# Expert outputs delivered to token order, and indirect DMAs in pairs by scan step, in a macaron block of mixture of experts and delta-rule attention

## The reference

```python
x = x + 0.5 * ffn(layernorm(x))
x = x + attn(layernorm(x))
x = x + 0.5 * ffn(layernorm(x))
```

```python
p, idx = top_k(softmax(x @ gate_w.T), 2);  p = p / sum(p)
for k in range(2):
    pos = place of the token in the queue of expert idx[:, k]   # by token number
    valid = pos < capacity                                      # 640
    disp = zeros(8, 640, 128) filled with the valid tokens
    y = (silu(disp @ wi_gate.T) * (disp @ wi_up.T)) @ wo.T      # hidden width 512
    out += where(valid, p[:, k] * y[idx, pos], 0)
```

## Time and profile before

| | |
|---|---|
| median of 3 runs | 1117.05 us (1116.97, 1117.05, 1122.63) |
| the profiled execution | 1120.73 us, of which its span is 1118.9 |
| mean granted TensorE clock | 0.898 of the full 2.4 GHz |
| busy PE / DVE / ACT / POOL | 854.6 / 543.9 / 335.9 / 465.5 us |
| routing | 0 to 75 us |
| `e1` | 75 to 299 us, PE busy 202.9, clock 0.97 |
| attention, stage -1 | 299 to 405 us |
| stages 0, 1, 2 | to 505, 610 and 715 us, PE busy 98 to 102 in each |
| stage 3 and the last routing | 715 to 845 us |
| `e2` | 845 to 1060 us, PE busy 201.1, clock 0.95 |
| `collect` | 1060 to 1119 us, DVE busy 17.2, POOL 39.5, PE none |

### The profile page before, as it was taken

How to read it: one execution, slowest core, us unless ns; L and a number is a source line. 1 busy time by engine, 2 the same in 40 slices (tenths; PEclk the granted TensorE clock), 3 DMA queues, 4 the chain that set the end, 5 groups by cost and what they waited for, 6 DMA issues and landing times. The chain is left out here.

```text
span 1118.9 us, 26929 instructions
## 1 busy us (share of the span) xinstructions
PE 854.6 (76%) x11563; PEld 751.8 (67%) x11563; DVE 543.9 (49%) x1569; ACT 335.9 (30%) x646; POOL 465.5 (42%) x588
## 2 busy tenths in 40 slices
PE   4419999969558579988998899797526999799800
PEld 3419999969546457776777678665415999799800
DVE  6715565625455024575566356622623555445333
ACT  2214444324122112342234325311413444334200
POOL 1664479842233820870185028302024420323076
PEclk9999999979868869999999999986656999989955
DMA  7333434523100000000000000000004434334113
GB/s 266 131 109 112 142 116 125 157 88 94 56 26 2 0 22 4 2 20 32 4 2 21 4 4 1 21 4 21 1 17 139 133 125 136 107 118 143 55 40 110
DMA packets 68467, 75.71 MB, mean 68 GB/s; under 512 B 8150, under 2 KB 55165, under 8 KB 67836
## 3 DMA queue, kind: packets, MB, share of 16 engines
q1 hardware_dynamic: 60156, 57.27, 16.2%
...
## 5 line engine op out<-in xcount | busy, mean ns | idle before, releaser
L237 POOL DMA_INDIRECT queue<-xn,slot x128 | 128.2, 1002 | 247.8 <-DVE slot L1459 104.7
L638 DVE TENSOR_TENSOR e_hid<-e_sg,e_pu 128x320 f32<-128x320 f32 x256 | 123.9, 486 | 195.8 <-ACT e_sg L594 134.1
L594 ACT ACTIVATE e_sg<-e_pg 128x320 f32<-128x320 f32 x256 | 111.6, 438 | 233.1 <-PE e_pg L556 162.4
L554 PE MATMUL e_pg<-e_xlo,e_whi 128*128 128x320 f32 x256 | 97.7, 382 | 23.6 <-issue 15.3
L243 POOL DMA_INDIRECT xn<-rows,slot x64 | 61.6, 963 | 123.2 <-ACT e_xhi L580 61.1
L684 POOL TENSOR_TENSOR a_prod<-a_inv,a_nmat 128x31 f32<-128x31 f32 (+15 forms) x124 | 64.5, 521 | 95.4 <-DVE a_nmat L1317 86.0
L541 PE MATMUL e_po<-expert,e_hid 128*128 128x128 f32 x640 | 86.2, 278 | 0.3 <-issue 0.3
L541 PE MATMUL e_po<-e_expert,e_hid 128*128 128x128 f32 x640 | 84.0, 276 | 1.3 <-DVE e_hid L638 1.3
L895 PE MATMUL a_pz<-a_vhi,lag_hi 128*128 128x512 f32 x184 | 79.3, 431 | 5.0 <-DVE a_vlo L1272 5.0
L541 PEld LDWEIGHTS e_po<-expert,e_hid 128*128 128x128 f32 x640 | 82.2, 194 | 0.5 <-issue 0.5
L541 PEld LDWEIGHTS e_po<-e_expert,e_hid 128*128 128x128 f32 x640 | 80.3, 193 | 1.8 <-DVE e_hid L638 1.8
...
## 6 DMA issues: line engine op xcount, KB each, us to landing
...
queue<-xn,slot POOLq DMA_INDIRECT x128
```

The costliest lines, as they stand in the source:

```text
L237: pool.indirect_dma_start(io.queue[c], bass.IndirectOffsetOnAxis(ap=k.slot[:, j, c:c + 1], axis=0), k.xn[:, j, :], None, bounds_check=SLOT ...
L554: pe.matmul(out, whi[par][:, i, fs], xlo[par][:, cols], start=True, stop=False)
L594: act.activation(sg[n % 2][:], pg[n % 2][:, 0:HALF], ACT.Silu).then_inc(silued, 1)
L638: dve.tensor_tensor(hid[q % 2][:, f, c * HALF:c * HALF + HALF], sg[n % 2][:], pu[n % 2][:, 0:HALF], ALU.mult).then_inc(hidden, 1)
```

## The change

**What it does.** The queue rows get a 129th number, the token's own number (less a constant, so that an empty slot, which holds zeros, is out of bounds). VectorE turns that column of `xs` into a table `token` for each pass (`index`). Where the next reader wants token order, `deliver` writes the expert's output rows by token number into `io.token[c]`, five indirect DMAs for a pass, and rows with a number out of bounds are skipped. In `e1` that is done for choice 1, in `e2` for both. They are read back by plain loads: four of 512 KB in attention, and eight at the end of `e2`. The choice-0 rows of `e1` still go to `io.rows` in slot order and are gathered: group 0 in `e1`, four tiles before pass 8's deliveries and four behind them, group 1 and 2 at the head of attention, group 3 in pairs in stage 0. `token[0]` and `token[1]` are zeroed by SP, as are the queues.

The folding of attention's weights is cut into pieces that stand between the groups of scatters in `e1`. In `e2` only the last group's eight choice-1 scatters are left in the loops; attention sends the other 24 along with choice 0. The last pass projects the pass before it down two blocks earlier, and its own first two tiles in between, each tile copied out by itself. The first inversion moves to VectorE. `collect` as a function goes; its adds and stores stand at the end of `e2`.

```diff
-def gather(pool, io, c, slot, dst, got):
-    pool.indirect_dma_start(dst, None, io.rows[c], bass.IndirectOffsetOnAxis(ap=slot, axis=0)).then_inc(got, 16)
+def gather(pool, io, slot, dst, got):
+    pool.indirect_dma_start(dst, None, io.rows, bass.IndirectOffsetOnAxis(ap=slot, axis=0)).then_inc(got, 16)
+def deliver(pool, io, c, token, src, stored):
+    pool.indirect_dma_start(io.token[c], bass.IndirectOffsetOnAxis(ap=token, axis=0), src, None,
+                            bounds_check=NTOK - 1, oob_is_err=False).then_inc(stored, 16)
...
-                clear(sp, 1, later)
-            sp.wait_ge(later, 16 * (1 + (len(loads) + CLEARS if raw else 0)))
+                for table in (io.queue[1], io.token[1], io.token[0]):
+                    clear(sp, table, later)
+                sp.dma_start(io.rows[SLOTS:SLOTS + 1, :], zero[0:1, 0:D]).then_inc(later, 16)
...
+                dve.tensor_copy(k.xn[:, :, D], k.const[:, C_TOKEN:C_TOKEN + NT])
...
-        SCATTERS = (0, 5, 10, 15, 20, 24, 28, NT)
+        SCATTERS = (0, 5, 10, 15, 20, 24, 28, NT) if raw else (NT - GRP, NT - GRP // 2, NT)
+        NSENT = SCATTERS[-1] - SCATTERS[0]
+        LAST = NQ - 1
+        BY_TOKEN = (1,) if raw else (0, 1)
...
+            def collect(c, g):
+                own = slice(g * GRP, (g + 1) * GRP)
+                dst = second[:, own, :] if c else k.xn[:, own, 0:D]
+                sp.dma_start(dst, io.token[c].rearrange("(n p) d -> p n d", p=P)[:, own, :]).then_inc(got[c][g // 2 if c else 0], 16)
...
+                    if q == LAST:
+                        if n < CT:
+                            down(q - 1, n)
+                        elif n < CT + 2:
+                            down_last(n - CT)
+                    elif q and n in DOWN_AT:
                         down(q - 1, DOWN_AT.index(n))
-            for s in range(CT):
-                down(NQ - 1, s)
+            for s in range(2, CT):
+                down_last(s)
...
+            def index(q):
+                dve.tensor_scalar(token[:, q, :], xs[q % 2][:, :, D], float(NUMBERED), None,
...
+                if raw and i == 1:
+                    raw.fold_taps(pool, k, folded)
+                if raw and i == 2:
+                    raw.split_taps(pool, k, folded)
+                if raw and i == 3:
+                    raw.split_gates(pool, k, stacked)
+                if raw and i == 4:
+                    raw.fold_far(pool, k)
+                if raw and i == 5:
+                    raw.fold_near(pool, k)
...
+            def send_rows(q):
+                c = q // E
+                pool.wait_ge(indexed, numbered(q))
+                for s in range(CT):
+                    pool.wait_ge(rready, 2 * q + (s if q == LAST else s // 4) + 1)
+                    deliver(pool, io, c, token[:, q, s:s + 1], rows[q % 2][:, s, :], stored[c][q % 2])
...
+            pool.wait_ge(sent, 16 * NSENT)
+            if raw:
+                all_stored(pool, 0)
+                fetch(0, GRP // 2)
+            for q in range(NQ):
+                if q // E in BY_TOKEN:
+                    send_rows(q)
+                if raw and q == E:
+                    fetch(GRP // 2, GRP)
...
+            rows = io.token[1].rearrange("(n p) d -> p n d", p=P)
+            for a in range(NGRP):
+                own = slice(a * GRP, (a + 1) * GRP)
+                sp.dma_start(k.xn[:, own, 0:D] if a else second, rows[:, own, :]).then_inc(loaded[min(a, 1)], 16)
...
             fetch(1)
-            for g in range(-1, NGRP):
-                if g + 1 < NGRP:
-                    invert(g + 1)
-                if g >= 1:
-                    send(g - 1)
-                if g + 3 < NGRP:
-                    fetch(g + 3)
-            send(NGRP - 1)
-            pool.wait_ge(sent, 16 * NT)
+            fetch(2)
+            invert(0)
+            for j in range(4):
+                in_step(0, j + 1)
+                fetch(3, 2 * j, 2 * j + 2)
+            invert(1)
+            invert(2)
+            for j in range(4):
+                in_step(2, j)
+                send(0, 0, 2 * j, 2 * j + 2)
+                behind_read(2, j + 1)
+                send(0, 1, 2 * j, 2 * j + 2)
+            invert(3)
+            for j in range(4):
+                in_step(3, j)
+                send(1, 0, 2 * j, 2 * j + 2)
+                behind_read(3, j + 1)
+                send(1, 1, 2 * j, 2 * j + 2)
+            for j in range(4):
+                in_step(3, j + 4)
+                send(2, 0, 2 * j, 2 * j + 2)
+                if j < 3:
+                    behind_read(3, j + 5)
+                    send(2, 1, 2 * j, 2 * j + 2)
+            send(2, 1, 6, GRP)
+            send(NGRP - 1, 0)
...
+            def invert_first(first, last):
+                dve.wait_ge(subchain, 2)
+                dve.wait_ge(factored, 1)
+                substitute(dve, link, nmat, inv, prod, first, last)
+                if last == CHUNK - 1:
+                    dve.sem_inc(inverted, 1)
...
+                if ahead and not here and n == 4:
+                    low_values(a, 0)
+                    low_values(a, 1)
+                    invert_first(0, 12)
+                    cross_values(a)
+                    invert_first(12, CHUNK - 1)
...
-            for a in range(NGRP):
-                combine(a, 0)
+            link(dve.tensor_scalar(k.xn[:, :, D], k.xn[:, :, D], -float(APART), None, ALU.add))
+            combine(0, 0)
...
+        self.queue = [scratch(f"queue{c}", SLOTS, ROW) for c in range(TOPK)]
+        self.rows = scratch("rows", SLOTS + 1, D)
+        self.token = [scratch(f"token{c}", NTOK, D) for c in range(TOPK)]
```

261 lines of the change are left out of this document (158 added, 103 removed).

## The result

The changed kernel takes **1087.18 us** (median of 4, 1085.01 to 1089.70) where the kernel before takes 1117.82 beside it. The ratio is 0.9711, 95% interval 0.9683 to 0.9739. The forecast was 1040, its range 1020 to 1066. The profiled execution took 1089.70 with a span of 1087.7, 31.2 less than the 1118.9 of before.

A forecast was written before the change was run, and what follows sets the result against it. Bound: TensorE in the experts, stalled under long rows of indirect DMAs, then 32 gathers at the end. -23 - 3 - 20 - 4 - 28 + 1.4 = -76.6 from 1120.73: 1044.1; that execution lay 3.7 above median, so 1040, range 1020 to 1066.

The forecast's parts named there:

- Four places, one pattern: Both expert phases, a scan read in attention and two solves: long rows of indirect DMAs run TensorE dry, 4 to 12 us in.
- Five in a row, 6.5 us, cost nothing: Expert passes: five scatters in a row leave TensorE busy 11.83 of 12 us, so they cost nothing.
- D: Attention: last stage's burst goes, scatters stand in pairs by scan step; -4 us, bounds -8 and +20.
- A: Experts' interiors: both 16-bursts go, five deliveries per by-token expert replace them; -13.05 - 8.96 - 2.10 + 1 = -23 us.
- F: Queue rows of 516 bytes instead of 512: first load of each expert phase grows; 2 x 0.7 = +1.4 us.
- B: First experts to attention: next stage starts 4.1 us later, but attention's head gets shorter; -3 us together.
- E: Tail: 32 gathers and their wait go; deliveries, plain loads and adds replace them, one delivery held; -28 us.
- The head: Start of attention: one 512 KB load replaces waiting for eight gathers; adds done at 311.0 against 313.86.
- C: First inversion moves to VectorE (-11), two solves no longer under gathers (-8), less time at 1.2 GHz (-1); -20 us.
- pairs starve the scan: Rival, 15%: 48 scatters in attention's scan steps lose 24 us at half the old burst's rate, giving 1062; at all, 1084.
- the better case: Rival, 20%: tail deliveries not held (5.7 us), stage 3 loses nothing (4 more), a little from bursts; 1026.
- It decides from 2.4 us for a delivery: Rival, slower, 2%: GpSimd bounds the 24 delivering experts, 120 us per us above that; at 3.1 all 77 is lost.

The follow-up runs named there:

- e1: Not a follow-up run: the kernel's first expert phase (sublayer), which ends where attention begins; no measured time of its own as a run.

## Why the prediction was wrong

**What bounds the kernel.** "Four places, one pattern: a long unbroken row of indirect DMAs, and TensorE runs dry some 4 us into it": the pattern was seen rightly in that trace, and it is real in the late condition. Two things in it were wrong. It is the other engines that take up TensorE's results late, which the rows of the changed kernel show, so an engine can be hit with large instructions and in a short row. And "Five in a row, 6.5 us, cost nothing" was read from a busy share of 11.83 in 12 us. From the first scatter of that row, at 109.89, to the first of the next, at 122.59, it is 12.70 in the same trace, and the next pass, with four, 12.02. A busy share over a window doesn't see a wait that lies just outside it.

**Where the 45 us went** that were forecast and not gained: 25 in the four stages (D), 17 in the expert phases (A and F), 8 at the end of `e1` (B), against 6 that the tail gave more than forecast (E).

**A, -23 forecast, -4.3 with F.** The step that failed is "five deliveries, 6.5 us in 12.0, as the scatters have now at no cost". The 13.05 and the 11.06 did go. So did 2.3 of before that I hadn't seen (two passes with five scatters, 12.7 each, and one of 12.99 beside the folding). In their place came ten passes of `e2` over 12.03 by 0.72 to 1.13 (8.5 together), two like them in `e1` (1.5), the nine DMAs in a row (a pass of 16.6, 4.6 where I charged 1), and the folding's subtraction on VectorE (4.9, and 1.8 in the pass behind), which I had put at nothing since no engine waited for GpSimd there. For `e1` alone these make -1.9, measured are -1.7. I had checked who waits for the folding's result, not which instruction beside it may have to wait. In the calm condition 13.05 and 11.06 aren't there to be gained: the passes take 12.0 in both kernels.

**B, the phase end, +4.1 forecast, +11.8.** From the last delivery to the next phase it takes 9.3 for my 2.8, which is 6.5 of the 7.7 too little; 1.0 is the last delivery's wait for its late tile. The calm traces have the 6.5 as well (+10.6), so it belongs to the change in either condition. **The head, -7.1, and C, -20:** measured -26.6, each part within 1.5. In the calm condition it is -19.1, as the solves weren't delayed there before.

**D, -4 forecast, +21.2 in the four stages.** By size this is the largest miss. The step that failed is "a pair takes 2.6 us, under the 4 us at which TensorE ran dry". This was the rival "pairs starve the scan", which I gave 15% and 24 us where I have 4 (that makes 1060, not the 1062 written). By its parts: stage 2 +4.8, the scan of stage 3 +7.5, what follows it +4.4, and 4.4 in stages 0 and 1, which is another cause. Of the 7.5, two steps with pairs grew by 5.1 and one by 5.0 at a lower clock, which varies between traces of either kernel, while the step that held the eight scatters fell by 1.6. That it is the pairs that cost in stages 2 and 3 is read from these rows and from the calm traces, where the same code has +0.4 in stage 2 and -2.1 in the scan of stage 3; no kernel without them ran in the late condition. As for stages 0 and 1, the adds that leave the head are made there, and I priced their leaving and not their coming. That cost stands in the calm condition too, +4.8 of the +5.1.

**E, -28 forecast, -33.8.** The hold of a delivery under the adds was right in size; it is in every calm trace with the 32 adds in a row, at 6.23 to 6.25 us in eleven of thirteen and at 4.95 and 7.05 in the others. In the late one the copies themselves came so late that nine of ten deliveries were out before the adds began and none was held. That is the 5.7 of the better case, by luck, since its reason for an unheld tail was another. **F, +1.4:** the sum had it for the first load of each phase, which cost next to nothing (to TensorE's first transpose 3.15 us instead of 3.23 in `e1`, 3.08 instead of 2.95 in `e2`). It is the second load's transposes in `e2` that stand 1.4 later behind the first load (9.11 instead of 7.66), so the number is right by luck. The prediction's 24 beats, from the Trainium skill (DMA: Bandwidth & Descriptors, How a descriptor splits into AXI transactions), hold for the row with the worst start; rows 516 bytes apart take 17 to 24 by that page, an estimate of some 20 on average.

**The range** left out that two cases could come together: the bursts as the cause, and their successors as the next. "It decides from 2.4 us for a delivery" looked for the cost in GpSimd's own time, where it never was.

**What stays open:** what the late condition is (it came and went between sessions, in each of which it held for the kernel before as well), whether a fifth DMA, the loads beside it or something else made the 12.75, what the pairs alone cost attention in the late condition, and what takes the 8 us between GpSimd's last indirect DMA and the next phase.
